# GpSimd pauses behind every four transfers, landing waits go, and the first edge sum starts in slot 12 of pass 2

## What is computed

```python
xn = layernorm(x)
# L0: the first edge sum, weighted by edge_weight (and the degrees), then two products with batch norms
agg = segment_sum(xn[src], dst)                      # 100000 rows of 256
x = x + gnn0(agg) + mixer0(xn)                       # mixer0: 4 layers of linear attention + feed-forward
x = x + moe(layernorm(x))                            # 8 experts, top 2
xn = layernorm(x)
# L1: the second edge sum, by edge softmax over the other end of the edges
x = x + segment_sum(att * h[col], row) + mixer1(xn)  # row = src, col = dst
x = x + chosen_tokens_ffn(x)
```

## Time and profile before

| | us |
|---|---|
| median of 3 runs | 6614.56 (6593.85 to 6631.38) |
| profiled execution | 6644.69, of which its span 6642.9 |
| mean granted TensorE clock | 0.912 |

### The profile page before, as it was taken

How to read it: one execution, slowest core, us unless ns; L and a number is a source line. 1 busy time by engine, 2 the same in 40 slices (tenths; PEclk the granted TensorE clock), 3 DMA queues, 4 the chain that set the end, 5 groups by cost and what they waited for, 6 DMA issues and landing times. The chain is left out here.

```text
span 6642.9 us, 86982 instructions
## 1 busy us (share of the span) xinstructions
PE 5500.2 (83%) x25856; PEld 4557.9 (69%) x25856; DVE 3337.6 (50%) x8788; ACT 2922.0 (44%) x7114; POOL 3305.5 (50%) x3346
## 2 busy tenths in 40 slices
PE   4578998889988888788887899997678787778799
PEld 2457877777877777667766687876446666566688
DVE  8555666334444444333323554544556666666551
ACT  6333444444545454444443333332435444544444
POOL 1565665654255655555553556562225555555200
PEclk8789999999999999889998899998778989988899
DMA  2212112121233332333344221222223333333511
GB/s 75 70 46 61 45 41 63 36 68 50 76 95 89 86 85 83 97 87 104 99 93 103 88 56 48 54 54 61 78 58 92 93 93 94 97 92 93 89 42 35
DMA packets 378185, 493.01 MB, mean 74 GB/s; under 512 B 97664, under 2 KB 315640, under 8 KB 375288
## 3 DMA queue, kind: packets, MB, share of 16 engines
q0 software_dynamic: 135008, 236.92, 15.0%
q1 hardware_dynamic: 242712, 250.54, 12.8%
HBM read 385.16 MB, written 102.04 MB: 73 GB/s over the span
## 5 line engine op out<-in xcount | busy, mean ns | idle before, releaser
L302 POOL DMA_INDIRECT edges_g<-xn_rows,edges_idx x880 | 875.7, 995 | 791.2 <-issue 315.4
L2043 POOL DMA_INDIRECT messages_g<-h_rows,edges_record x880 | 835.8, 950 | 743.7 <-PE messages_s_ps L2213 449.7
L246 POOL DMA_INDIRECT sorted_dst<-edges_record,edges_place x784 | 795.2, 1014 | 633.0 <-DMA sorted_dst<-edges_record,edges_place 269.2
L246 POOL DMA_INDIRECT sorted_src<-edges_record,edges_place x784 | 770.9, 983 | 595.8 <-issue 225.2
L1230 PE MATMUL mixer_y_ps<-mixer_w,mixer_g 128*125 128x256 f32 x3200 | 788.4, 401 | 122.9 <-ACT mixer_g L1376 121.3
L1230 PEld LDWEIGHTS mixer_y_ps<-mixer_w,mixer_g 128*125 128x125 f32 x3200 | 629.1, 200 | 233.4 <-ACT mixer_g L1376 133.0
L1219 PE MATMUL mixer_f_ps<-mixer_f_out,mixer_w 128*128 128x250 f32 x3200 | 768.4, 384 | 12.7 <-ACT mixer_g L1376 6.4
L1219 PEld LDWEIGHTS mixer_f_ps<-mixer_f_out,mixer_w 128*128 128x128 f32 x3200 | 614.6, 196 | 87.3 <-issue 7.9
L2213 PE MATMUL messages_s_ps<-messages_g,messages_one 128*128 128x257 f32 x1760 | 514.4, 440 | 150.0 <-issue 83.0
L2213 PEld LDWEIGHTS messages_s_ps<-messages_g,messages_one 128*128 128x128 f32 x1760 | 363.3, 217 | 243.0 <-issue 110.7
L1376 ACT ACTIVATE mixer_g<-mixer_f_ps,mixer_b 128x250 f32<-128x250 f32 x800 | 329.8, 465 | 320.9 <-PE mixer_f_ps L1219 194.4
(11 more groups left out here) (542 smaller groups left out, 10428.2 us busy)
## 6 DMA issues: line engine op xcount, KB each, us to landing
mixer_q<-qT SPq DMA_DIRECT2D x100, 250.0 KB
mix_rows<-mixer_rows SPq DMA_DIRECT2D x100, 250.0 KB
qT<-mixer_qT SPq DMA_DIRECT2D x75, 250.0 KB
mixer_rows<-mix_rows SPq DMA_DIRECT2D x75, 250.0 KB
edges_g<-xn_rows,edges_idx POOLq DMA_INDIRECT x880
messages_g<-h_rows,edges_record POOLq DMA_INDIRECT x880
sorted_dst<-edges_record,edges_place POOLq DMA_INDIRECT x784
sorted_src<-edges_record,edges_place POOLq DMA_INDIRECT x784
```

The costliest lines, as they stand in the source:

```text
L246: self.nc.gpsimd.indirect_dma_start(self.orders[s][0], bass.IndirectOffsetOnAxis(self.place[s][:, j:j + 1], 0), self.record[s][:, j, :], N ...
L302: self.nc.gpsimd.indirect_dma_start(self.g[n % GR][:, j, 0:D], None, self.table_d, bass.IndirectOffsetOnAxis(self.idx[:, t:t + 1], 0)).the ...
L2043: self.nc.gpsimd.indirect_dma_start(self.g[n % GR][:, j, :], None, self.table_d, bass.IndirectOffsetOnAxis(self.idx[:, t:t + 1], 0)).then_inc(
```

## The change

1. `pool_pause`: five memsets of a 128x96 tile that nobody reads (`edges_idle`), each of which waits for the one before on GpSimd's own semaphore. It stands behind every four scatters and every four gathers of the first sum; 612 pauses, 3060 memsets. The second sum's gathers have none.
2. Waits: a scatter waits at each four for the landing of the four two back, in place of all earlier ones at each eight. A gather waits no longer for the landing of the batch before. `pool_spread_landed` and the wait for the batch in front of a share are gone.
3. `share`: the first sum begins in slot 12 of pass 2 with one batch per slot (14 batches in pass 2 in place of 8); pass 3 has 1 and 2 in turn in its first 12 slots and then 2 (46 in place of 52); pass 4 is as before (50).
4. `share_of`: 64 scatters behind batch 4 as before, then 8 behind each of 9, 12, ... 42 (12 shares in place of 21), in all 160 in place of 232. The message layer gets 80 in place of 64, the experts 544 in place of 488.

```diff
+PAUSES = 5
+        self.idle, self.idled, self.pauses = sb(keep, "idle", [P, 96]), nc.alloc_semaphore("edges_idled"), 0
     def pool_spread_first(self, pool, j0, j1):
         for j in range(j0, j1):
             four = j // FOUR
-            if j % (2 * FOUR) == 0 and j:
-                for b in range(2):
-                    pool.wait_ge(self.scattered[b], 16 * FOUR * (four // 2))
+            if j % FOUR == 0 and four >= 2:
+                pool.wait_ge(self.scattered[four % 2], 16 * FOUR * (four // 2))
             self.pool_scatter(pool, 0, j, self.scattered[four % 2])
+            if j % FOUR == FOUR - 1:
+                self.pool_pause(pool)
+    def pool_spread_second(self, pool, j0, j1):
...
+    def pool_pause(self, pool):
+        for _ in range(PAUSES):
+            if self.pauses:
+                pool.wait_ge(self.idled, self.pauses)
+            self.nc.gpsimd.memset(self.idle[:, :], 0.0).then_inc(self.idled, 1)
+            self.pauses += 1
     def pool_gather(self, pool, n):
-        if n:
-            pool.wait_ge(self.landed[(n - 1) % GR], 32 * PB * ((n - 1) // GR + 1))
         for j in range(2 * PB):
...
+            if j % FOUR == FOUR - 1:
+                self.pool_pause(pool)
-    in_message = 64
-    share = [[0] * (NCH + 1), [0] * 21 + [1, 1, 2, 2, 2], [2] * (NCH + 1), [2] * NCH + [0]]
+    in_message = 80
+    share = [[0] * (NCH + 1), [0] * 12 + [1] * 14, [1, 2] * 6 + [2] * 14, [2] * NCH + [0]]
-    share_of = {n: 2 * FOUR for n in range(9, 72, 3)}
+    share_of = {n: 2 * FOUR for n in range(9, 45, 3)}
     share_of[GR - 1] = 16 * FOUR
-                    pool.wait_ge(edges.landed[n % GR], 16 * 2 * PB * (n // GR + 1))
-                    edges.pool_spread_eights(pool, until[n] - share_of[n], until[n])
-                    edges.pool_spread_landed(pool, until[n])
+                    edges.pool_spread_second(pool, until[n] - share_of[n], until[n])
```

More of the change, by code:

```diff
@@ L259, in pool_spread_first @@
             pool.wait_ge(self.scattered[b], 16 * (ET // 2))
-    def pool_spread_eights(self, pool, j0, j1):
+    def pool_spread_second(self, pool, j0, j1):
         for j in range(j0, j1):
             four = j // FOUR
[L264 to L267, removed]
+            if j % FOUR == 0 and four >= 2:
+                pool.wait_ge(self.spread[four % 2], 16 * FOUR * (four // 2))
             self.pool_scatter(pool, 1, j, self.spread[four % 2])
[L270 to L273, removed]
+            if j % FOUR == FOUR - 1:
[6 more added lines that the diff above has]
+            self.pauses += 1
     def pool_list_second(self, pool, rec):
@@ L2536, in _ @@
         def _(pool):
-            edges.pool_spread_eights(pool, *spread)
-            edges.pool_spread_landed(pool, spread[1])
+            edges.pool_spread_second(pool, *spread)
         @block.sync
@@ L2754, in _ @@
         def _(pool):
-            edges.pool_spread_eights(pool, spread, ET)
+            edges.pool_spread_second(pool, spread, ET)
             for b in range(2):
```

## The result

The changed kernel takes **6277.28 us** (median of 4, 6271.42 to 6294.19) against 6622.97 us of the kernel before (6593.85 to 6660.42) beside it: ratio 0.948, interval 0.943 to 0.953. Forecast was 6519, range 6400 to 6680. The sign was right, the gain is three and a half times as large. The profiled execution took 6294.19 us, 350 less than that of before. I call *hold* what the prediction calls so: VectorE and ScalarE sit idle over finished work while GpSimd issues transfers. This pair ran when there were holds; at other times there were none, and the ratio is then another (see the table of sittings).

What follows compares the result with a forecast made beforehand. No engine was full; holds beside GpSimd's transfers slowed TensorE's stages, and GpSimd bound pass 3. Terms +60 (pass 2), -116 (pass 3), -40 (pass 4), +3 (message layer), -3 (experts) gave -96: 6519 us, range 6400 to 6680.

Steps and rivals of the forecast that it cites:

- A four ... 6.6: GpSimd: four transfers with their pause take 6.5 us, or 6.6 with the first scatter's lengthened issues; ends 6.4 and 7.4.
- Each 0.1 us costs 40 us: Some 400 fours of GpSimd stand on the path, so each 0.1 us more per four costs 40 us.
- How much of the holds goes ... I take half: Holds are halved: 2.4 us saved per block of pass 2, 1.7 in the experts; ends nothing and all 4.8.
- Opening, pass 1, pass 2 to the first sum: nothing gained: ScalarE reaches slot 11 of pass 2 near 1375 us, then waits some 100 us for the first gathers: gain gone.
- GpSimd is now last: Experts: GpSimd's scatters and lists take 917 us and end last, so -3 us instead of -37.
- Pass 3: With 46 batches instead of 52, bound by TensorE: 834 us against 950, so -116.
- Pass 4: GpSimd takes 26.4 us per slot; with holds halved each slot saves 1.6 us, so -40.
- The second sum: The last stage, whose gathers get no pause: untouched, 0 us.
- The removed waits cost nothing elsewhere: Landing waits: the new one is asked for some 8 us behind the last issue it waits for, so no cost.
- The rest is longer: Rival, 0.20: gap of 0.2 us between memsets makes a four 7.1 us: +200, 6748 us, or 6717 by the median.
- The holds don't shrink: Rival, 0.12: the 1.7 us pause is too short and issues renew holds: +19, 6633 us, no change.
- GpSimd faster, holds gone: Rival, 0.18: a four of 6.4 us and holds cut by three quarters: some -230, 6386 us.

Runs made afterwards that it cites:

- no_pause_again: The changed kernel without rests (PAUSES = 0), in a sitting with holds: 8051.78 us, 1.244 of the kernel before.
- old_shares_again: The changed kernel with the first sum's shares of before (from slot 21 of pass 2), in a sitting with holds: 6128.21 us, 0.948 of the kernel before.
- old_shares: The changed kernel with the first sum's shares of before (from slot 21 of pass 2), in a sitting without holds: 5960.3 us, 0.954 of the kernel before.
- pauses_2: The changed kernel with two memsets behind every four transfers in place of five, in a sitting with holds: 7900.44 us, 1.223 of the kernel before.
- pause_at_eight: The changed kernel with its five memsets behind every eight transfers in place of four, in a sitting with holds: 7775.28 us, 1.204 of the kernel before.

## Why the prediction was wrong, point by point

Two terms of the sum were mis-sized, and each is worth about half of the 254 us by which the sum of -96 missed the -350 of the profiled executions. The split is my estimate from the stages.

- **"A four ... 6.6" and "eight are then 13.2 us, what eight cost today" is the first step that failed.** Measured 4 x 1.59 = 6.36 in the first scatter and 6.18 in the experts, so eight are 12.7 and 12.4: GpSimd became faster, where I had left it as it was. A memset took 0.186 us where I had 0.21, the gap 43.0 / 935 = 0.05 where I took 0.08, the first transfer behind a pause started after 0.16 and not 0.30; and for the experts I used the 6.6 of the first scatter where my own working gave 6.5. The price: GpSimd sets when the first and the sixth batch are there, so some 60 us up to the sixth batch; some 45 in pass 4 (24.6 us for its 16 transfers per slot, not 26.4); over the 136 fours of the experts 0.42 us each are 57 us, of which some 35 would have shown with the holds halved. In all some 140 us. "Each 0.1 us costs 40 us" in the prediction says the same.
- **"How much of the holds goes ... I take half" is the second.** My upper end, all 4.8 us per block, was the truth in pass 2. I had a hold begin anywhere in a stretch of issues and end 1.8 us behind it; that model left 3.1 of 5.6, and the blocks of pass 2 up to the first sum show none left. It knew neither a rate nor a limit to the run. The experiments show both: it depends on how fast transfers come in the mean and on the length of a run (1.37 to 1.41 us per transfer: a standstill; 1.62 in eights: mild; 1.61 in fours: next to nothing). The 67 us of attend and 52 of pass 1 are holds that went, but they bought nothing: ScalarE spent them waiting in slot 11. What counted is some 24 us between the sixth batch and the end of pass 2, 56 in pass 3, some 30 in pass 4 and 15 in the experts: some 125 us.
- **"Opening, pass 1, pass 2 to the first sum: nothing gained" was right in form.** ScalarE arrived in slot 11 at 1419.2 - 126.8 = 1292 us, not 1375, and waited 127, not some 100: the gain in front of it was indeed given back there. But the lists came 50 us earlier than I had them (last scatter at 1395.4, not about 1446), and the sixth batch cost 33 us, near the 38 of the forecast. Pass 2 ended at 1830, not 1920.
- **"GpSimd is now last" in the experts is not what happened.** Its lists were ready 13 us before the others were done.
- **Pass 3**: TensorE's as I said, 778 us, not 834: 30.4 us in slots with two batches (I had 32.6), 28.1 in the mean of one and two (30.7). Both are my sums without the 2.4 us of hold. **Pass 4**: GpSimd's bound of 16 transfers per slot became the real one in most slots: the first six blocks come 23 us apart, those behind them about 25, and 16 x 1.54 is 24.6.
- **The second sum** stayed as it was, as said: +3.
- **"The removed waits cost nothing elsewhere"** was true beside long enough pauses only. The waits for landing were the kernel's rest before; without either it takes 8050 us under holds. I named no rival in which the waits mattered, and that is the largest effect in this case.
- **The rivals.** "The rest is longer" was wrong in sign (6.2, not 7.1). "The holds don't shrink" is false here. "GpSimd faster, holds gone" at 6386 had both terms in the right direction, and stopped at a four of 6.4 and three quarters of the holds. My range ended at 6400, above that rival's own 6386.
- The Trainium skill, "SBUF — State Buffer", section "Who interferes with whom", says that PE and ACT never wait on anyone; it speaks of SBUF ports. The rows of no_pause_again show ScalarE idle 31.8 us at a step between engines, while GpSimd issues. By that rule the rests would have bought nothing; the trace disagrees for what passes between engines, and no run here speaks on the ports themselves. (Of the 12.73 us of the earlier trace rows, 9.9 lie behind the end of the product, 4661.94 - 4652.08; the prediction counts them all.)

## What to carry over

Behind a stream of small indirect transfers on GpSimd look at engines that stop together, and count microseconds per transfer and the length of a run before taking any wait away: a wait that looks idle may be the pacing. A pause behind short runs paced more cheaply here than waiting for landings (old_shares_again 0.948, old_shares 0.954), and is worth testing with none, some and many, since too few gave nothing at all under holds. And time such a change in more than one sitting: here one kernel, the changed one without its rests, was worth -7% in one and +24% in another. And when two terms go into a forecast, give each its own error: here both erred the same way.

## What the runs showed that I had not expected

- The time of one program depends on the sitting, by 6% for the kernel before (6240 to 6623) and 38% without rests (5825 to 8052), while executions within a sitting agree to about 1%. What differs between sittings no run here can tell; two sittings under the same chip number differed.
- What is held seems to be the signal, not only the transfer. In pauses_2 GpSimd's second memset waits for the signal of its own first one, and now and then starts long after that one has ended (10 `remote` waits, up to 3.8 us, in the 210 to 1160 stretch; most gaps are short). Its timeline:

```profile
301.44 0.20 POOL L277 MEMSET edges_idle<- 128x96 f32 x1
303.41 0.18 POOL L277 MEMSET edges_idle<- 128x96 f32 x1 [1.77 <-remote]
303.75 0.97 POOL L248 DMA_INDIRECT sorted_dst<-edges_record,edges_place  x1 [0.16 <-issue]
...
308.51 0.20 POOL L277 MEMSET edges_idle<- 128x96 f32 x1
309.70 0.18 POOL L277 MEMSET edges_idle<- 128x96 f32 x1 [0.99 <-issue]
```

  1.77 and 0.99 us where the changed kernel's gap is 0.05 in the mean. Each transfer here raises a semaphore by 16. That such increments queue ahead of the engines' own signals would fit a rate and a run length; it is argued, not shown, since no run changed the number of increments per transfer. The 25 transfers of no_pause_again are no fixed limit: in the first scatter the longest `remote` waits of VectorE and ScalarE are 24.1 us in pause_at_eight and 29.8 in pauses_2, some 17 and 21 transfers, and in the experts of no_pause_again they reach 66.4.
- In no_pause_again a held-up VectorE came back to GpSimd as a wait of 732 us through one early semaphore, so a stall on one engine outlived the transfers that had caused it.
